# Softplus of the time step in a Mamba kernel: the sum moves from VectorE to TensorE, and seven due slots move with it

## The reference

```
xz = x @ W_in ; xh, z = split(xz)
xh = silu(causal_conv_k2(xh, conv_w, conv_b))
x_dbl = xh @ W_x                      # dt_low (8), B (16), C (16)
dt = softplus(dt_low @ W_dt + b_dt)   # 256 channels
h = exp(dt * A) * h + dt * B * xh     # scan over 4096 positions, 256 x 16 states
y = sum_n(h * C) + xh * D
out = (y * silu(z)) @ W_out
```

## Time and profile before

| | |
|---|---|
| median of 3 runs | 14091.14 us (14086.54 to 14091.33) |
| the profiled execution | 14087.19 us, span of its instructions 14085.4 us |
| mean granted TensorE clock | 0.814 of full speed |
| PE, PEld busy | 10270.4 us (73%), 2928.6 us (21%) |
| DVE busy | 13484.2 us (96%) |
| ACT busy | 12153.5 us (86%) |
| POOL busy | 13256.8 us (94%) |
| DVE scans, line 933 | 8192, 9457.3 us |
| DVE softplus, line 892 | 256, 309.6 us |
| DMA | 2177.48 MB, 16 engines 65.6% |

### The profile page before, as it was taken

The page is one execution under the profiler, slowest core; times in us unless marked ns, Lnnn a source line. Parts: engine busy times, 40 slices in busy tenths (PEclk is TensorE's granted clock), DMA queues, the critical chain, the costliest instruction groups (busy, mean ns, idle before and its releaser), DMA issues.

```text
span 14085.4 us, 171990 instructions
## 1 busy us (share of the span) xinstructions
PE 10270.4 (73%) x34752; PEld 2928.6 (21%) x34752; DVE 13484.2 (96%) x12084; ACT 12153.5 (86%) x24809; POOL 13256.8 (94%) x3076
## 2 busy tenths in 40 slices
PE   6777777777777777777777777777777777777776
PEld 1222222222222222222222222222222222222221
DVE  7999999999999999999999999999999999999999
ACT  7888888888888888888888888888888888888888
POOL 6999999999999999999999999999999999999999
PEclk8788888888888888788888888888888888888887
DMA  6666666666666666666666666666666666666665
GB/s 145 158 150 158 153 163 152 154 154 157 158 154 158 151 160 154 158 155 154 155 157 161 150 160 149 160 156 155 157 151 160 155 157 153 156 154 160 154 152 126
DMA packets 1195314, 2177.48 MB, mean 155 GB/s; under 512 B 152321, under 2 KB 161594, under 8 KB 1194042
## 3 DMA queue, kind: packets, MB, share of 16 engines
q1 hardware_dynamic: 1192762, 2164.07, 65.6%
q10 hardware_dynamic: 1280, 0.02, 0.0%
HBM read 1811.17 MB, written 352.32 MB: 154 GB/s over the span
## 4 chain that ended last, share of the span: by engine, by line
POOL 51%; issue 33%; DVE 5%; ACT 4%; PE 3%; DMA 2%; SPq 1%; POOLq 0%; ACTq 0%; DVEq 0%
POOL hq L1047 36%; POOL dbx L1037 15%; DVE hq L933 3%; ACT ps_a L631 1%; DMA dt_d<-dt 1%; DMA b_rep<-bc_d 1%; DVE dbx L916 1%; PE pp L427 1%; DMA dtx_d<-sp 1%; ACT L756 0%; PE pp L395 0%; DVE pp L892 0%; ACT dbx L645 0%; PE pp L396 0%; PE ps_acc L451 0%
## 5 line engine op out<-in xcount | busy, mean ns | idle before, releaser
L1047 POOL TENSOR_TENSOR hq<-hq,c_rep 128x2048 f32<-128x2048 f32 x2048 | 9254.6, 4534 | 718.5 <-ACT carry L650 717.5
L933 DVE TENSOR_TENSOR_SCAN hq<-ps_a,dbx 128x512 f32<-128x512 f32 x8192 | 9457.3, 1207 | 364.2 <-ACT dbx L645 219.7
L631 ACT ACTIVATE ps_a<-dt_rep,A_neg 128x512 f32<-128x512 f32 x8192 | 5625.3, 687 | 1396.3 <-DVE hq L933 1323.1
L1037 POOL TENSOR_TENSOR dbx<-dtx_rep,b_rep 128x2048 f32<-128x2048 f32 (+1 forms) x1024 | 4076.8, 3981 | 88.9 <-DMA dtx_rep<-dtx_d 88.9
L645 ACT ACTIVATE dbx<-ps_a,dbx,carry 128x1 f32<-128x1 f32 x7168 | 2501.0, 349 | 169.0 <-POOL dbx L1037 64.1
L916 DVE TENSOR_TENSOR dbx<-dtx_rep,ps_b 128x2048 f32<-128x2048 f32 (+1 forms) x1280 | 2625.7, 2051 | 8.2 <-PE ps_b L439 8.2
L451 PE MATMUL ps_acc<-hq,dsum 128*32 128x512 f32 x16384 | 2352.1, 648 | 112.3 <-POOL hq L1047 111.4
L427 PE MATMUL pp<-y,w_Wout 128*128 128x512 f32 x1024 | 935.2, 1068 | 1389.2 <-ACT dt L671 1388.4
L439 PE MATMUL ps_b<-dbl,bsel 41*128 41x512 f32 x2560 | 1555.3, 690 | 356.6 <-issue 199.3
L395 PE MATMUL pp<-x,W_taps 128*128 128x512 f32 x768 | 725.3, 1046 | 870.0 <-DVE x L887 579.2
L448 PE MATMUL ps_acc<-xh,D_diag 128*128 128x512 f32 x1024 | 634.4, 704 | 177.1 <-DVE y L903 176.0
(11 more groups left out here) (123 smaller groups left out, 10109.1 us busy)
## 6 DMA issues: line engine op xcount, KB each, us to landing
dtx_rep<-dtx_d SPq DMA_DIRECT2D x2048, 256.0 KB, 5.3
dt_rep<-dt_d SPq DMA_DIRECT2D x2048, 256.0 KB, 5.8
c_rep<-bc_d SPq DMA_DIRECT2D x1024, 256.0 KB, 4.7
xr<-in_x SPq DMA_DIRECT2D x704, 256.0 KB, 10.6
b_rep<-bc_d SPq DMA_DIRECT2D x2048, 64.0 KB, 5.6
dtx_d<-sp SPq DMA_DIRECT2D x256, 512.0 KB, 2.8
dt_d<-dt SPq DMA_DIRECT2D x256, 512.0 KB, 6.0
xin<-in_x SPq DMA_DIRECT2D x256, 256.0 KB, 9.6
```

Of the source, the lines that this page charges most:

```text
L631: A(ps_a[:, BANK[i], :], dt_rep[:, q // NQ, g, :], ACT.Exp, scale=A_neg[:, q // NQ, q % NQ, g:g + 1]).then_inc(exp_done, 1)
L933: v.tensor_tensor_scan(hq[:, q % HQ, g, :], ps_a[:, BANK[i], :], dbx[:, slot(q), g, :], 0.0, ALU.mult, ALU.add).then_inc(scan_done, 1)
L1037: g.tensor_tensor(dbx[:, slot(q), m:, :], dtx_rep[:, d, m:, :], b_rep[:, q % NQ // 2, :].unsqueeze(1).to_broadcast([P, DG - m, T]), ALU.mu ...
L1047: g.tensor_tensor(quad, quad, c_rep[:, c % 2, q % NQ, :].unsqueeze(1).to_broadcast([P, DG, T]), ALU.mult).then_inc(cmul_done, 1)
```

## The change

On TensorE, softplus becomes two accumulations in PSUM. `W_dt` and `b_dt` are halved once at the start, so that `step_dt` leaves a/2. |a/2| is added to it with the unit matrix as weights, which makes max(a, 0), and then the logarithm in the same way. DVE's softplus instruction goes; Exp gets the scale -2 and writes `dt` instead of `sp` (and so has the wait for the store of the chunk before that `evac_dt` had), Ln works in `dt`.

The slots: the two new steps are on PE in slots 14 and 16; `dt_x` on DVE moves from 16 to 18, `evac_dt` on ACT from 17 to 19, `step_y` from 19 to 20, `step_out` from 18 to 21 (now behind `step_y`), GELU from 21 to 22, DVE's `gate` from 23 to 24, `step_gc`, `square`, `step_var` and `rstd` one slot later each, and the gate of half 1 (`DVE_Y1`) from 9 to 8.

```diff
-PE_XH, PE_Z, PE_DBL, PE_DT, PE_OUT = (1, 2), (3, 5), 7, 10, 18
+PE_XH, PE_Z, PE_DBL, PE_DT, PE_OUT = (1, 2), (3, 5), 7, 10, 21
+PE_STEP = (14, 16)
 PE_CONV = (11, 12, 13)
-PE_Y, PE_GC, PE_VAR = 19, 24, 27
-ACT_XZ, ACT_DBL, ACT_SP, ACT_DT, ACT_OUT = 5, 9, (12, 13, 14), 17, 23
-ACT_CONV, ACT_GELU, ACT_SQ, ACT_RSTD = 18, 21, 26, 29
-DVE_NORM, DVE_Y1, DVE_DT, DVE_Y0, DVE_GATE = 0, 9, 16, 24, 23
+PE_Y, PE_GC, PE_VAR = 20, 25, 28
+ACT_XZ, ACT_DBL, ACT_SP, ACT_DT, ACT_OUT = 5, 9, (12, 13, 14), 19, 23
+ACT_CONV, ACT_GELU, ACT_SQ, ACT_RSTD = 18, 22, 27, 30
+DVE_NORM, DVE_Y1, DVE_DT, DVE_Y0, DVE_GATE = 0, 8, 18, 24, 24
...
+            def step_sum(b, c, k):
+                pe.wait_ge(sp_done, 3 * (b * CH + c) + (1, 3)[k])
+                for d in range(DI):
+                    last = mm(pp[:, d, :], w["ident"][:], (sp, dt)[k][:, d, :], start=False, stop=True, skip_group_check=True)
+                if k:
+                    last.then_inc(step_done, 1)
...
+                        for k in range(2):
+                            if u == PE_STEP[k]:
+                                step_sum(b, c + 1, k)
...
                     if k == 1:
-                        A(sp[:], sp[:], ACT.Exp, scale=-1.0).then_inc(sp_done, 1)
+                        if not (isinstance(b, int) and b * CH + c == 0):
+                            act.wait_ge(dt_out, 16 * (b * CH + c))
+                        A(dt[:], sp[:], ACT.Exp, scale=-2.0).then_inc(sp_done, 1)
                     else:
-                        A(sp[:], sp[:], ACT.Ln, bias=1.0).then_inc(sp_done, 1)
+                        A(dt[:], dt[:], ACT.Ln, bias=1.0).then_inc(sp_done, 1)
...
             def evac_dt(b, c):
                 act.wait_ge(dtx_done, b * CH + c + 1)
-                if not (isinstance(b, int) and b * CH + c == 0):
-                    act.wait_ge(dt_out, 16 * (b * CH + c))
                 A(dt[:], pp[:, 0:2, :], ACT.Copy).then_inc(dt_done, 1)
...
+            v.tensor_scalar(w["wdt"][:], w["wdt"][:], 0.5, None, ALU.mult)
...
-            def softplus(b, c):
-                dve.wait_ge(sp_done, 3 * (b * CH + c + 1))
-                v.scalar_tensor_tensor(pp[:, 0:2, :], pp[:, 0:2, :], 0.0, sp[:], ALU.max, ALU.add).then_inc(step_done, 1)
...
                         if u == DVE_DT:
-                            softplus(b, c + 1)
                             dt_x(b, c + 1)
```

More of the change, by code:

```diff
@@ L516, in _ @@
             step_dt(0, 0)
+            step_sum(0, 0, 0)
+            step_sum(0, 0, 1)
             for kw in (1, 0, 2):
@@ L1004, in _ @@
             add_input(0, 0)
-            softplus(0, 0)
             dt_x(0, 0)
```

## The result

| | median | runs | profiled execution | DVE, POOL, ACT, PE busy |
|---|---|---|---|---|
| before | 14089.81 us | 4 | 14087.19 us, span 14085.4 us | 96, 94, 86, 73% |
| changed | 14246.25 us | 4 (14245.8 to 14250.73) | 14246.05 us, span 14244.2 us | 93, 93, 86, 77% |

The account below looks back on a forecast made before the run. DVE was taken as the bound, ACT's slots 21 to 24 close behind. Per image 4 x 1.13 + 3 x 0.19 + 2.1 = 7.2, minus 3.0 for the gate, +4.2 us; times 32, +134 us: 14225 us, 8-in-10 range 14040 to 14310.

Parts of the forecast that it names:

- Softplus off DVE: Softplus instruction before `dt_x` leaves DVE: 1.24 us less per chunk.
- The hold on `dt_x`: DVE waits 0.7 us in each chunk before `dt_x` for PE's second unit-matrix pair.
- GELU behind scan 22: GELU in ACT's slot 22 waits for scan 22: +1.13 us in four odd chunks, +0.19 in three even.
- X': End of scan 16 with the stall before scan 9 covered, 0.35 us earlier in c=7; times count from it.
- The new order, y ahead of the output: On PE, y before `step_out` takes away GELU's wait in c=6; GELU wants y only at X' + 12.9.
- `group_stats`: In chunk c=8 it waits for `evac_out`: +1.7 us, and +0.4 on `group_scale`, together +2.1.
- The gate in slot 8: Gate of half 1 fills DVE's stall before scan 9, up to 0.58 us in seven chunks: -3.0 us per image.
- The DMA side: Stores and spreads behind `dt_x` come 1.7 us later; nothing is late, with 2.8 us to spare.
- Rival A: PE doesn't hold `dt_x`: 5.6 us per image come off, 14046 us; chance 0.12.
- Rival B: DVE's time alone decides, ACT catching up: about 1.0 us per chunk gained, 13835 us; chance 0.10.
- Rival D: The change doesn't reach the bound, two effects cancelling: within 0.2% of 14091 us; chance 0.06.
- Rival C: PE's clock is slow in slots 14 to 16: 3.4 us more per chunk, 15095 us; chance 0.04.

Follow-up runs that it names:

- e3: Changed kernel with one pair of unit-matrix matmuls instead of two, the logarithm left out of the sum; 14105.8 us, ratio 1.0013.
- e5: Changed kernel with the second unit-matrix sum in PE's slot 15 instead of 16, ahead of `select_b`; 14099.42 us, ratio 1.0009.
- e1: Changed kernel with GELU back in ACT's slot 21, all else as changed; 14076.59 us, ratio 0.9993.
- e2: Kernel before, softplus left on DVE, with six later slots alone (GELU, gate, center, square, variance, rstd); 14483.86 us, ratio 1.0283.
- e7: The kernel of e6 with `rstd` in ACT's slot 29 instead of 30; 13944.31 us, ratio 0.9899 against the kernel before.
- e4: Changed kernel with the gate of half 1 back in slot 9; 14251.99 us, ratio 1.0119.
- e8: Kernel before with the gate of half 1 in slot 8 instead of 9, nothing else; 14049.8 us, ratio 0.9973.
- e6: Changed kernel with the edits of e1 and e5 both made; 13972.76 us, ratio 0.9919.

## Why the prediction was right, step by step

**Softplus off DVE.** 278 us less busy time on DVE, 1.09 us per chunk: busy time counts 1.21 for softplus less overlap; the 1.24 of the text are place to place. Right.

**The hold on `dt_x`.** Forecast 0.7 us in each chunk; measured 0.33 in c=1 to 4, 0.55 to 0.57 in c=5 to 7, 0.66 in c=8, 3.65 us per image instead of 5.6. The mechanism was right and the term too large. The price of a pair was right to 0.03 us. DVE takes 2.34 us from scan 17 to `dt_x` and not 2.27. In c=1 to 4 it also stands idle for 0.16 us before scan 17, which the working hadn't. PE's row starts 0.07 us (c=5 to 7) and 0.16 us (c=1 to 4, beside that idle time) earlier against DVE than reckoned. e3 and e5 show that the hold counted in full.

**GELU behind scan 22.** Forecast: both tables back 4.0 us after scan 22, waits of 0.9 and 0.9 before scans 25 and 26, scan 26 at X' + 17.41. Measured in c=6: 0.91 and 0.88; scan 26 at 7092.27, which is 14.43 behind the start of `dt_x` (forecast 17.41 - 2.98 = 14.43). The same 14.43 us stand in 212 of the 222 chunks with an `add_carry` and a GELU (14.42 to 14.43), so this chain sets scan 26 nearly everywhere. e1 shows the cause by undoing it; e2 has the same two waits without the sum on TensorE, in every such chunk. The wait before scan 9 is gone in all chunks, as forecast. No drain stands behind a table load here either: 7088.48 + 1.28 = 7089.76, and `add_carry` starts at 7089.78.

**The new order, y ahead of the output.** It does what the text says of GELU, which waits 3.3 us in all for y, 151.2 before. Its other side was missed: the gate of slot 24 waits for PE, 181.1 us in all. It costs almost nothing of its own, since the same time comes off the waits before scans 25 and 26: the three together are 1.7 to 1.8 us in the mean in each of c=1 to 7, in c=6 0.26 + 0.62 + 0.88 = 1.76, and 12.5 us per image, where the forecast had 7 x 1.8 = 12.6 for the two scans alone. Only in ten chunks of the whole execution does the gate's wait push scan 26 beyond the 14.43 us, by 0.2 to 0.3 us each, 2.5 us in all. In one of them, a chunk of c=3, PE's clock is slow for a part of the row: y, the output and the sum took from 6917.43 to 6925.03, and the gate waited 2.12 us; the granted clock from 6917 to 6925 us is 0.60.

```profile
6917.43 2.05 PE L385 MATMUL pp<-sq,w_b1T 128*128 128x512 f32 x2 [3.44 <-ACT dt L684]
6919.27 1.91 PE L386 MATMUL pp<-sq,w_b2T 128*128 128x512 f32 x2
6920.97 3.07 PE L435 MATMUL pp<-y,w_Wout 128*128 128x512 f32 x4
6923.97 1.06 PE L459 MATMUL ps_acc<-hq,dsum 128*32 128x512 f32 x8
```

The prediction hadn't looked at who waits for PE behind the two moved steps; that this hardly cost anything was luck.

**`group_stats`.** Forecast +1.7 us on its slot and +0.4 on `group_scale`; its total wait went up to 71.5 us in 32 cases, one of 5.2 at the kernel's end and 2.1 a time in the others, where the earlier trace rows has 0.24, and `group_scale` waits 0.58. Right, 0.4 us too small in sum.

**`rstd` and `make_diag`.** Missed: 51.6 us of wait, 1.5 per image. In slot 30 of c=5 ACT has other work, and the prediction has no term for the move of `rstd` at all. e7 gave 28 us of it back.

**The gate in slot 8.** Counted as -3.0 us per image. In the changed kernel it is worth 6 us in all, near the noise (e4), in the kernel before 37 us (e8), not 96. The forecast's sum is not wrong by this, since the hold on `dt_x` was reckoned against a DVE that is early by it; but the two terms stood as if they were separate, and the term by itself was too large by the factor 2.6.

**The sum.** Forecast +4.2 us per image; measured (14244.2 - 14085.4) / 32 = +5.0. DVE's waits by chunk and slot, in the mean of 29 images of the loop, show that the missing 0.8 is what is left of larger errors. Too little was reckoned for `rstd` (1.5), the wait before scan 17 (0.6), `att_weights` in c=4 (0.55; why it grew is not shown) and the group norm (0.4), 3.05 in all; too much for the hold (1.95), and the gain before scan 9 was 0.2 larger than reckoned. That the forecast lies within 21 us of the result is in part luck: the mechanisms were right, but 98 us that it had not were offset by 62 us that were not there. The DMA side was right: ACT waits 30.7 us in all for the spread dt (6.9 before), and scan 0 waits no longer than before.

**The rivals.** Rival A (no hold) is what e5 is: the forecast for it, 14046, is 53 us below e5's 14099; 21 of these it has from the sum, the rest is that the hold gave 147 us and not 179. Rival B, that DVE's time alone decides, didn't happen in the changed kernel: 278 us less work, 156 us slower. The Trainium skill, Perfetto Trace Analysis, Identifying the Most-Contended Engine, says to optimize the engine with the highest occupancy first; this trace doesn't bear out that such work pays by itself. With other slots e7 is 143 us faster than the kernel before, a bit over half of the 256 us that B gave. How much of it is the relief and how much the slots is not shown: no run has e7's slots with softplus left on DVE, and e8 gave 37 us by a slot alone. Rival D (no change) is excluded by the interval, 1.0095 to 1.013. Rival C is excluded: the pairs' 2048 instructions take 620 ns in the mean, and the granted clock from 7072 to 7078 us, where they stand in c=6, is 1.00 (the view of windows: PE, PEld, DVE, ACT, POOL busy, then the clock).

```profile
7072.00:7078.00 6.00, 6.00 (x26) 1.82 (x21) 5.45 (x6) 5.40 (x11) 6.00 (x3) 1.00 0.39 79
```

## What to carry to other kernels

Where queues are ordered by hand, cost a step by what stands in front of it and behind it in its queue: here one due slot (21 to 22) lost the cover of a 2.2 us multiplication and cost 170 us, and one matmul pair behind a step that nobody needed yet cost 147 us (undone together, 273). Read for each moved instruction the condition of the instruction just ahead of it; a move by one slot can pass a wait for work that is two steps longer. When an engine that is 96% busy is relieved, reckon the next wait at its old place before the gain is counted, and count a gap that is closed ahead of a wait only once.

## What the runs showed of the hardware that was not expected

TensorE's accumulation onto a bank that holds an earlier result costs the same as a plain matmul: a pair 1.98 us with `start=False`, 1.99 for Z. The mean granted clock of TensorE rose with the change, from 0.814 before to 0.855. It isn't the added work alone: with half of it (e3) the clock is 0.853, with the same work and GELU in slot 21 (e1, e6) 0.871, and with the kernel before's work in later slots (e2) 0.802. What keeps it up is not shown.
